# Second attention of a two-layer transformer kernel: the key mask from a table and a bias, the row loads in halves

## The chip, the cores and the metric

One core of one Trainium2 chip runs the whole program in one launch. The metric is the device time of an execution in microseconds (us), the median of several runs.

## The reference

The input is 16 batches of 128 tokens of width 128 (float32), a context of the same shape and a key mask of 16 x 128 integers. Two layers follow one another. Cut to the second attention, which the change is about:

```python
Q = (layernorm(x) @ Wq)   # 16 heads of 8 columns each
K, V = ctx @ Wk, ctx @ Wv
scores = einsum('bhqd,bhkd->bhqk', Q, K) / sqrt(8)
scores = where(mask[:, None, None, :] == 0, -inf, scores)
scores = where(triu(ones, k=1), -inf, scores)        # causal
x = x + einsum('bhqk,bhkd->bhqd', softmax(scores), V) @ Wo
```

Layer 0 is a cross attention without any mask, with biases, and a mixture of 8 experts (two chosen per token) on an RMS-normed input. Layer 1 is the attention above and a feed-forward part with ternary weights and inputs rounded to 8 bits. The drawn mask is all ones.

## The kernel before

Five blocks stand one after the other, each with its own instruction streams for the five engines, and all engines meet between two blocks: `context` (layer 0's projections), `attention` for layer 0, `experts`, `attention` for layer 1 (the second attention), and `ternary_ffn`.

**Rows.** Queries and keys are float32 values split into three bf16 parts. The keys' and queries' parts are stored to DRAM (`k_dram`, `q_dram`) and read back per batch as 72 partition rows (`PRODUCTS`: 3 x 3 parts x 8 columns) into one of four slots (`SLOTS`) of `k_rows` and `q_rows`, for all 16 heads. Rows 96 to 98 hold ones on the keys' side and, on the queries' side, the negated row maxima, which `lay_maxima` (L795) writes by a DMA from `neg_t`. In layer 1 row 72 (`ROW_MASK`) of `k_rows` is the batch's key mask (0 or -1e30 in bf16), which `load_rows` (L116 to L131) fetches by a third DMA from `mask_dram` (L130), against a row of ones in `q_rows` that ACT's queue writes once in `context` (L703). Everything else of the rows is zero.

**One batch of the attention.** It goes in four units q of four heads. `scores` (L852) waits for the batch's rows, then TensorE multiplies 96 rows of `q_rows` and `k_rows` per head into `ps_s` (queries in partitions, L867); in layer 1 a matmul of 512 columns first puts the causal triangle `upper` into the bank (L863). VectorE takes the negated maximum of each query (`maxima`, L957) and splits it in three bf16 parts (`split`, L964 to L970); TensorE turns them (L905), ACT copies them to `neg_t` (L1051), and SP lays them into the rows. Two steps later `shifted_scores` (L884) multiplies all 128 rows the other way round (keys in partitions) into `ps_e`; for units 1 and 3 of layer 1 a matmul with `lower` goes first (L880), for units 0 and 2 GpSimd clears the triangle afterwards (`causal`, L1101). ACT takes the exponential (L1039), TensorE multiplies with the values (`values`, L898), whose tile `v_aug` GpSimd fills (L1092).

**Order of the work.** Step b of an attention does `scores` of batch b+2 beside `shifted_scores` of batch b, unit by unit, and the values of batch b-1. The first and last steps are written out, and steps 6 to 13 are a loop of two turns with four steps each, in which b is a register (all engines but SP in layer 1, whose queue is written out in full). SP's queue per batch is in `load`: in layer 0 it waits for two units of the slot's last user, loads eight heads with two DMAs (`load_half`), waits for the other two units, loads the other half, then lays the maxima of batch b-2. In layer 1 it waits for all four units of batch b-4 (L804), issues keys, queries and mask (L125, L126, L130) and then lays the maxima.

**Experts.** Four groups of four batches, eight experts each. In group 0 TensorE also projects the second attention's keys and values from `ctx_t`, whose last use this is; GpSimd, VectorE and SP split and store the keys (L1208, L1266, L143). In groups 1 to 3 the second attention's queries are made in between: VectorE's statistics of the group (L187, L91 to L101), GpSimd's root (`queries.root`, L195), VectorE's normalising after expert 2 (L200), TensorE's turn after expert 3 (L206). SP then stores the queries of group 0 and loads the rows of the first four batches. All engines work in their order.

Of the kernel before, what the change touches and what calls it, by code (L numbers as in the profile page):

```python
# [14 lines left out]
B = 16  # L15
# [24 lines left out]
ROW_MASK = PRODUCTS  # L40
# [64 lines left out]
def load_half(sp, c, b, r, half):  # L105

    heads, rows_in = slice(half * H // 2, (half + 1) * H // 2), c["rows_in"][half]
    rows, queries = c["k_dram"][0, bass.ds(b, 1)], c["q_dram"][0, bass.ds(b, 1)]
# [7 lines left out]


def load_rows(sp, c, layer, b, r):

    k_rows, q_rows, rows_in = c["k_rows"], c["q_rows"], c["rows_in"][layer]  # L120

    rows, queries = c["k_dram"][layer, bass.ds(b, 1)], c["q_dram"][layer, bass.ds(b, 1)]
    windows = bass.AP(tensor=rows.tensor, offset=rows.offset,
                      ap=[[H * P, PARTS * DK], [DK * H * P, PARTS], [1, H * P]])
    sp.dma_start(k_rows[0:PRODUCTS, r].rearrange("p h t -> p (h t)"), windows).then_inc(rows_in[r], 16)  # L125
    sp.dma_start(q_rows[0:PRODUCTS, r].rearrange("p h t -> p (h t)"),  # L126
                 bass.AP(tensor=queries.tensor, offset=queries.offset,
                         ap=[[H * P, PARTS * DK], [0, PARTS], [1, H * P]])).then_inc(rows_in[r], 16)
    if layer == 1:
        sp.dma_start(k_rows[ROW_MASK:ROW_MASK + 1, r],  # L130
                     c["mask_dram"][bass.ds(b, 1)].unsqueeze(1).to_broadcast([1, H, P])).then_inc(rows_in[r], 16)  # L131
# [256 lines left out]
def main_kernel(nc, t):  # L388
    with ExitStack() as ctx:
        def sb(name, shape, dt):  # L390
# [19 lines left out]
            "ctx_t": sb("ctx_t", [P, T], F32),  # L410

# [14 lines left out]
            "rows_in": [[ctx.enter_context(nc.semaphore(f"rows_in{layer}_{r}")) for r in range(SLOTS)]  # L426
                        for layer in range(2)],
# [7 lines left out]
        c["xr"] = c["tokens"].tk  # L435
        context(nc, t, c)
# [6 lines left out]
def context(nc, t, c):  # L443
# [4 lines left out]
    with ExitStack() as ph:  # L448
# [11 lines left out]
        mask_i, mask_b = sb("mask_i", [B, P], I32), sb("mask_b", [B, P], BF16)  # L460
        one_rows = sb("one_rows", [H, SLOTS * P], BF16)
# [33 lines left out]
        def _(sp):  # L495
# [8 lines left out]
            sp.dma_start(mask_i[:], t["mask"]).then_inc(mask_in, 16)  # L504
            for layer, m in ((0, 3), (1, 0), (1, 1), (1, 2), (1, 3)):
                load_w(sp, layer, m, late_in)
# [9 lines left out]
            for b in range(AHEAD):  # L516
                for half in range(2):
                    load_half(sp, c, b, b, half)
# [611 lines left out]
def experts(nc, t, c):  # L1130
# [6 lines left out]
    with ExitStack() as ph:  # L1137
# [44 lines left out]
        def _(sp):  # L1182
# [12 lines left out]
            for b in range(SLOTS):  # L1195
                load_rows(sp, c, 1, b, b)
# [591 lines left out]
```

## Time and profile before

| | us |
|---|---|
| median of 3 runs | 437.22 (437.04 to 439.81) |
| the profiled execution, its own time | 438.72 |
| its span in the profile | 437.0 |
| TensorE matmul busy | 356.5 (82%) |
| VectorE busy | 288.8 (66%) |
| ACT busy | 224.7 (51%) |
| GpSimd busy | 89.9 (21%) |

Busy times are sums over the span of 437.0 us; the 1.7 us between the span and the execution's own time lie before and after what the profile records. Matmuls overlap their weight loads, so that both columns (PE and PEld) can be busy at once. A wait is the idle time of an engine in front of an instruction, put down to what released it. The granted clock of TensorE was 0.93 of full speed in the mean.

### The profile page before, as it was taken

What the parts mean: (1) busy time and instruction counts of PE and PEld (TensorE: products, weight loads), DVE (VectorE), ACT (ScalarE), POOL (GpSimd) and SP (SyncE); (2) the same over time, 40 slices, a digit from 0 to 9 for tenths busy, and PEclk for the clock granted to TensorE, in tenths of its full rate; (3) what the DMA queues carried; (4) which work ended last, traced back from release to release, by engine and by line L of the source; (5) the groups of instructions that cost most, each with busy time, mean ns of one, the idle gap of its engine ahead of it and who ended that gap; (6) DMA issues with size and microseconds to landing.
All of it is one profiled execution on the core that took longest, in us unless ns stands there. A gap on an engine that the chain in (4) does not pass through costs nothing. (4 is left out here: it accounts for less than half of the span.)

```text
span 437.0 us, 10507 instructions
## 1 busy us (share of the span) xinstructions
PE 356.5 (82%) x3434; PEld 256.6 (59%) x3434; DVE 288.8 (66%) x905; ACT 224.7 (51%) x420; POOL 89.9 (21%) x163
## 2 busy tenths in 40 slices
PE   1484677888977999999999999789899999757663
PEld 0352556766763567776677767557677676534442
DVE  5675677988965753574433443696789899367893
ACT  2142345656664664444434343146566656648894
POOL 6335040020203002100101001124333342310000
PEclk9887599999998999999999999889999999856997
DMA  7555864334317000650161100103444331000111
GB/s 200 119 145 126 209 162 129 118 113 119 97 30 240 2 1 5 127 111 1 35 179 41 36 0 0 37 14 108 132 124 113 96 103 29 3 1 1 32 30 37
DMA packets 54100, 34.98 MB, mean 80 GB/s; under 512 B 38744, under 2 KB 46256, under 8 KB 54064
## 3 DMA queue, kind: packets, MB, share of 16 engines
q1 hardware_dynamic: 44032, 31.43, 26.7%
q10 hardware_dynamic: 10032, 3.08, 3.0%
q8 instruction: 20, 0.33, 0.3%
q14 instruction: 16, 0.13, 0.1%
HBM read 24.60 MB, written 9.44 MB: 78 GB/s over the span
## 5 line engine op out<-in xcount | busy, mean ns | idle before, releaser
L1039 ACT ACTIVATE probs<-ps_e 128x512 f32<-128x512 f32 x128 | 75.5, 594 | 60.7 <-PE ps_e L884 55.9
L957 DVE TENSOR_REDUCE neg<-ps_s 128x4 f32<-128x512 f32 x128 | 85.2, 685 | 23.3 <-PE ps_s L867 22.1
L1285 DVE SCALAR_TENSOR_TENSOR x_all<-ps_ym,c_g,x_all 128x128 f32 (+1 forms) x128 | 36.0, 344 | 63.1 <-PE ps_ym L1380 63.0
L1380 PEld LDWEIGHTS ps_ym<-w,hid 128*128 128x128 f32 x512 | 60.8, 192 | 9.2 <-issue 6.7
L1380 PE MATMUL ps_ym<-w,hid 128*128 128x128 f32 x512 | 62.2, 276 | 0.0
L1370 PE MATMUL ps_h<-tok_t,w 128*128 (+1 forms) x128 | 61.9, 607 | 0.0
L1487 ACT ACTIVATE hid<-ps_h,b 128x512 f32<-128x512 f32 x64 | 43.1, 684 | 35.3 <-PE ps_h L1370 33.9
L867 PE MATMUL ps_s<-k_rows,q_rows 96*128 96x128 bf16 x512 | 54.0, 233 | 8.7 <-PEq L448 3.9
L884 PE MATMUL ps_e<-q_rows,k_rows 128*128 128x128 bf16 x512 | 50.6, 224 | 11.0 <-DMA q_rows<-neg_t 10.3
L867 PEld LDWEIGHTS ps_s<-k_rows,q_rows 96*128 96x128 bf16 x512 | 40.1, 104 | 22.2 <-issue 9.6
L884 PEld LDWEIGHTS ps_e<-q_rows,k_rows 128*128 128x128 bf16 x512 | 36.2, 100 | 17.7 <-DMA q_rows<-neg_t 10.1
L898 PE MATMUL ps_pv<-probs,v_aug 128*32 128x128 f32 x1024 | 36.4, 284 | 0.0
L1370 PEld LDWEIGHTS ps_h<-tok_t,w 128*128 128x128 f32 x128 | 22.5, 195 | 20.1 <-issue 14.9
L1092 POOL TENSOR_TENSOR v_aug<-v_all,zero 128x128 f32<-128x128 f32 x32 | 14.5, 455 | 92.8 <-PE ps_pv L898 92.2
L863 PE MATMUL ps_s<-upper,identb 128*128 128x512 bf16 x64 | 25.8, 404 | 5.1 <-PEq L1137 2.0
L898 PEld LDWEIGHTS ps_pv<-probs,v_aug 128*32 128x32 f32 x1024 | 26.9, 113 | 4.1 <-issue 0.4
L1051 ACT ACTIVATE neg_t<-ps_n 48x128 bf16<-48x128 bf16 x32 | 8.6, 269 | 32.2 <-PE ps_n L905 32.2
L924 PE MATMUL ps_y<-attn_w,oo_t 128*128 128x128 f32 x64 | 15.8, 330 | 9.7 <-ACT oo_t L1056 9.1
L1717 PE MATMUL ps_tf<-ident,gr 128*128 128x128 f32 x64 | 11.8, 313 | 14.0 <-ACT gr L1671 14.0
L983 DVE TENSOR_TENSOR x_all<-ps_y,x_all 128x128 f32<-128x128 f32 (+1 forms) x32 | 9.2, 288 | 17.7 <-PE ps_y L924 17.3
L1101 POOL TENSOR_SCALAR_AFFINE_SELECT probs<-probs 128x512 f32<-128x512 f32 x32 | 20.0, 625 | 0.0
L1044 ACT ACTIVATE o_t<-ps_pv 128x512 f32<-128x512 f32 x32 | 18.6, 580 | 2.0 <-PE ps_pv L898 1.9
(200 smaller groups left out, 552.5 us busy)
## 6 DMA issues: line engine op xcount, KB each, us to landing
k_rows<-k_dram SPq DMA_DIRECT2D x32, 144.0 KB
q_rows<-q_dram SPq DMA_DIRECT2D x32, 144.0 KB
k_rows<-k_dram SPq DMA_DIRECT2D x16, 288.0 KB
q_rows<-q_dram SPq DMA_DIRECT2D x16, 288.0 KB
k_dram<-parts SPq DMA_DIRECT2D x35, 128.0 KB, 2.3
w<-in_w SPq DMA_DIRECT2D x16, 128.0 KB, 2.6
q_dram<-parts SPq DMA_DIRECT2D x15, 128.0 KB, 2.2
q_dram<-parts ACTq DMA_DIRECT2D x9, 128.0 KB, 3.1
```

Source lines behind the costliest of these rows:

```text
L863: pe.matmul(ps_s[:, q % 2, :], identb[:], c["upper"][:].unsqueeze(1).to_broadcast([P, HQ, P]), start=True, stop=False, skip_group_check=True)
L867: last = pe.matmul(ps_s[:, q % 2, j * P:(j + 1) * P], q_rows[0:ROW_MAX, r, h, :], k_rows[0:ROW_MAX, r, h, :], start=(layer == 0), stop=Tru ...
L884: last = pe.matmul(ps_e[:, q % 2, j * P:(j + 1) * P], k_rows[:, r, h, :], q_rows[:, r, h, :], start=not masked, stop=True, skip_group_chec ...
L898: last = pe.matmul(ps_v[VW * j:VW * (j + 1), q * P:(q + 1) * P], v_aug[:, s, q * HQ + j, :], probs[:, s, q, j * P:(j + 1) * P], start=True ...
L957: dve.tensor_reduce(neg[:, s, q * HQ:(q + 1) * HQ], ps_s[:, q % 2, :].rearrange("p (h k) -> p h k", h=HQ), AX_X, ALU.max, negate=True).the ...
L1039: act.activation(probs[:, s, q, :], ps_e[:, q % 2, :], ACT.Exp, scale=SCALE).then_inc(exp_done, 1)
L1044: act.activation(o_t[:, s, :], ps_v[:], ACT.Copy).then_inc(ot_ready, 1)
L1101: pool.affine_select(out=probs[:, s, q, :], in_=probs[:, s, q, :], compare_op=ALU.is_ge, fill=0.0, base=0, pattern=[[0, HQ], [1, P]], chan ...
L1285: dve.scalar_tensor_tensor(out=batch_of(x_all, g * G + j), in0=ps_y[:, e % 2, j * D:(j + 1) * D], scalar=c_g[:, j, e:e + 1], in1=batch_of( ...
L1370: pe.matmul(ps_h[:, m, :], w1[:, e, m * P:(m + 1) * P], tok_t[:, bass.ds(g * GT, GT)], start=True, stop=True).then_inc(h_done, 1)
L1380: last = pe.matmul(ps_y[:, e % 2, j * D:(j + 1) * D], hid[:, (e % 2) * M + m, j * P:(j + 1) * P], w2[:, e, m, :], start=(m == 0), stop=(m ...
L1487: act.activation(hid[:, (e % 2) * M + m, :], ps_h[:, m, :], ACT.Gelu, bias=b1[:, e * M + m:e * M + m + 1]).then_inc(h_ready, 1)
```

## The change

The key mask no longer goes through the rows. In `context` the mask is also read turned round (`mask_t`, 128 keys x 16 batches) and VectorE makes `key_mask` of it (0 or -1e30 per key and batch); ACT's DMA of the row of ones into `q_rows` goes. In `experts`, when the projections have left `ctx_t`, SP fetches `mask_dram` broadcast to 128 partitions (2048 bf16 values in each) into its memory (`masks`) and GpSimd adds `upper` to all sixteen batches, ahead of the queries' part of its queue. In the second attention the matmul at L863 takes the batch's slice of that table instead of `upper`; GpSimd's `fill` copies the batch's column of `key_mask` to `key_bias`, and ACT's exponential takes this as its bias, for which it waits at unit 0. Row loads of layer 1 are done as in layer 0, in halves (four DMAs per batch instead of three), and TensorE waits for a half at units 0 and 2. The `scores` matmuls of both layers take 72 rows instead of 96. The semaphores `rows_in` are now per half; renamings of `rank_ready` are left out below.

```diff
-def load_half(sp, c, b, r, half):
+def load_half(sp, c, layer, b, r, half):
     heads, rows_in = slice(half * H // 2, (half + 1) * H // 2), c["rows_in"][half]
-    rows, queries = c["k_dram"][0, bass.ds(b, 1)], c["q_dram"][0, bass.ds(b, 1)]
+    rows, queries = c["k_dram"][layer, bass.ds(b, 1)], c["q_dram"][layer, bass.ds(b, 1)]
     first, many = half * H // 2 * P, H // 2 * P
...
-def load_rows(sp, c, layer, b, r):
-    k_rows, q_rows, rows_in = c["k_rows"], c["q_rows"], c["rows_in"][layer]
-    rows, queries = c["k_dram"][layer, bass.ds(b, 1)], c["q_dram"][layer, bass.ds(b, 1)]
-    windows = bass.AP(tensor=rows.tensor, offset=rows.offset,
-                      ap=[[H * P, PARTS * DK], [DK * H * P, PARTS], [1, H * P]])
-    sp.dma_start(k_rows[0:PRODUCTS, r].rearrange("p h t -> p (h t)"), windows).then_inc(rows_in[r], 16)
-    sp.dma_start(q_rows[0:PRODUCTS, r].rearrange("p h t -> p (h t)"),
-                 bass.AP(tensor=queries.tensor, offset=queries.offset,
-                         ap=[[H * P, PARTS * DK], [0, PARTS], [1, H * P]])).then_inc(rows_in[r], 16)
-    if layer == 1:
-        sp.dma_start(k_rows[ROW_MASK:ROW_MASK + 1, r],
-                     c["mask_dram"][bass.ds(b, 1)].unsqueeze(1).to_broadcast([1, H, P])).then_inc(rows_in[r], 16)
...
+            "key_mask": sb("key_mask", [P, B], F32),
...
-            "rows_in": [[ctx.enter_context(nc.semaphore(f"rows_in{layer}_{r}")) for r in range(SLOTS)]
-                        for layer in range(2)],
+            "rows_in": [[ctx.enter_context(nc.semaphore(f"rows_in{half}_{r}")) for r in range(SLOTS)]
+                        for half in range(2)],
...
+        c["masks"] = c["ctx_t"][:, 0:T // 2].bitcast(BF16).rearrange("p (b k) -> p b k", b=B)
...
             sp.dma_start(mask_i[:], t["mask"]).then_inc(mask_in, 16)
+            sp.dma_start(mask_t[:], t["mask_t"]).then_inc(mask_in, 16)
...
-                    load_half(sp, c, b, b, half)
+                    load_half(sp, c, 0, b, b, half)
-            sp.wait_ge(rows_set, 16 * (PARTS + 1))
+            sp.wait_ge(rows_set, 16 * PARTS)
...
             dve.tensor_copy(parts[:, FAST, 1], rest[:, FAST]).then_inc(fast_split, 1)
             dve.wait_ge(fast_split, 1)
             dve.tensor_tensor(parts[:, FAST, 2], rest[:, FAST], parts[:, FAST, 1], ALU.subtract).then_inc(fast_split, 1)
-            dve.wait_ge(mask_in, 16)
+            dve.wait_ge(mask_in, 32)
+            dve.tensor_scalar(c["key_mask"][:], mask_t[:], 0, MASKED, ALU.is_equal, ALU.mult)
             dve.tensor_scalar(mask_b[:], mask_i[:], 0, MASKED, ALU.is_equal, ALU.mult).then_inc(mask_ready, 1)
...
                         act.dma_start(k_rows[ROW_MAX + r:ROW_MAX + r + 1], one_rows[:]).then_inc(rows_set, 16)
-                    act.dma_start(q_rows[ROW_MASK:ROW_MASK + 1], one_rows[:]).then_inc(rows_set, 16)
...
+        key_bias, n_filled = sb("key_bias", [P, 2], F32), 1 + layer
-        n_loads = 2 if layer == 0 else 3
...
             def load(b, r):
-                if layer == 0:
-                    for half in range(2):
-                        sp.wait_ge(shifted, (b - SLOTS) * NQ + (half + 1) * NQ // 2)
-                        load_half(sp, c, b, r, half)
-                else:
-                    sp.wait_ge(shifted, (b - SLOTS + 1) * NQ)
-                    load_rows(sp, c, layer, b, r)
+                for half in range(2):
+                    sp.wait_ge(shifted, (b - SLOTS) * NQ + (half + 1) * NQ // 2)
+                    load_half(sp, c, layer, b, r, half)
                 lay_maxima(b - 2, (r - 2) % SLOTS)
...
             def scores(b, q, r):
                 n = b * NQ + q
-                if layer == 0 and q % 2 == 0:
-                    wait(pe, c["rows_in"][q // 2][r], of_slot(b, r, SLOTS, 16 * n_loads))
-                if layer == 1 and q == 0:
-                    wait(pe, rows_in[r], of_slot(b, r, SLOTS, 16 * n_loads) + 16 * 2 * B // SLOTS)
+                if q % 2 == 0:
+                    wait(pe, c["rows_in"][q // 2][r], of_slot(b, r, SLOTS, 16 * 2) + layer * (16 * 2 * B // SLOTS))
                 wait(pe, max_done, n - 1)
-                    pe.matmul(ps_s[:, q % 2, :], identb[:], c["upper"][:].unsqueeze(1).to_broadcast([P, HQ, P]),
+                    pe.matmul(ps_s[:, q % 2, :], identb[:], c["masks"][:, bass.ds(b, 1), :].to_broadcast([P, HQ, P]),
                               start=True, stop=False, skip_group_check=True)
                 for j in range(HQ):
                     h = q * HQ + j
-                    last = pe.matmul(ps_s[:, q % 2, j * P:(j + 1) * P], q_rows[0:ROW_MAX, r, h, :], k_rows[0:ROW_MAX, r, h, :],
+                    last = pe.matmul(ps_s[:, q % 2, j * P:(j + 1) * P], q_rows[0:PRODUCTS, r, h, :], k_rows[0:PRODUCTS, r, h, :],
                                      start=(layer == 0), stop=True, skip_group_check=True)
                 last.then_inc(scored, 1)
...
-                    wait(pe, vaug_ready, b + 1)
+                    wait(pe, vaug_ready, (b + 1) * n_filled)
...
                 wait(act, pv_done, n - 2 * NQ + 1)
-                act.activation(probs[:, s, q, :], ps_e[:, q % 2, :], ACT.Exp, scale=SCALE).then_inc(exp_done, 1)
+                if layer == 1 and q == 0:
+                    wait(act, vaug_ready, (b + 1) * n_filled)
+                masked = key_bias[:, s:s + 1] if layer == 1 else 0.0
+                act.activation(probs[:, s, q, :], ps_e[:, q % 2, :], ACT.Exp, bias=masked, scale=SCALE).then_inc(exp_done, 1)
...
             def fill(b, s):
                 wait(pool, pv_done, (b - 1) * NQ)
+                if layer == 1:
+                    pool.tensor_tensor(key_bias[:, s:s + 1], c["key_mask"][:, bass.ds(b, 1)], c["zero"][:, 0:1], ALU.add)\
+                        .then_inc(vaug_ready, 1)
                 pool.tensor_tensor(v_aug[:, s, :, 0:DK],
...
+            sp.wait_ge(v_done, NG)
+            sp.dma_start(c["masks"][:], c["mask_dram"].unsqueeze(0).to_broadcast([P, B, P])).then_inc(tables_ready, 16)
             queries.store(sp, 0, queries.stored[0])
             sp.wait_ge(queries.stored[0], 16 * PARTS)
             for b in range(SLOTS):
-                load_rows(sp, c, 1, b, b)
+                for half in range(2):
+                    load_half(sp, c, 1, b, b, half)
             queries.store(sp, 1, queries.stored[1])
-            pool.iota(rank_i[:], pattern=[[-1, E]], base=E, channel_multiplier=0).then_inc(rank_ready, 1)
-            pool.wait_ge(rank_ready, 1)
-            pool.tensor_copy(rank[:], rank_i[:]).then_inc(rank_ready, 1)
+            pool.iota(rank_i[:], pattern=[[-1, E]], base=E, channel_multiplier=0).then_inc(tables_ready, 1)
+            pool.wait_ge(tables_ready, 1)
+            pool.tensor_copy(rank[:], rank_i[:]).then_inc(tables_ready, 1)
                 pool.wait_ge(k_copied, 2 * (g + 1))
                 pool.tensor_tensor(k_rest[:, g], k_full[:, g], k_parts[:, g, 0], ALU.subtract).then_inc(k_rest_ready, 1)
+            pool.wait_ge(tables_ready, 2 + 16)
+            pool.tensor_tensor(c["masks"][:], c["masks"][:], c["upper"][:].unsqueeze(1).to_broadcast([P, B, P]), ALU.add)
             with pool.Fori(0, NG - 1) as g:
                 queries.root(pool, g)
                 queries.leave(pool, g)
...
-            dve.wait_ge(rank_ready, 2)
+            dve.wait_ge(tables_ready, 2)
...
-        "mask": mask_BxS2_if1,
+        "mask": mask_BxS2_if1, "mask_t": np.transpose(mask_BxS2_if1),
```

## Rows read from the trace of the kernel before

**Rows 1.** Windows: us, then PE, PEld, DVE, ACT, POOL busy; clock; DMA.

```profile
136.50:279.60 143.10, 139.82 (x788) 97.71 (x788) 71.33 (x258) 65.17 (x101) 13.27 (x13) 0.99 0.20 50
...
279.60:386.80 107.20, 94.55 (x1254) 69.05 (x1254) 82.86 (x257) 60.47 (x130) 37.87 (x88) 0.94 0.27 77
```

**Rows 2.** Waits of the second attention: total us, times, longest.

```profile
PE ps_s L863 <- DMA k_rows<-mask_dram: 1.7, 4, 0.8
...
PEld ps_s L863 <- DMA k_rows<-mask_dram: 1.2, 3, 0.5
```

**Rows 3.** Windows of single steps of the second attention, columns as in 1.

```profile
322.80:328.30 5.50, 5.27 (x78) 4.00 (x76) 5.19 (x20) 3.30 (x7) 2.20 (x6) 1.00 0.35 110
...
339.80:346.20 6.40, 5.54 (x80) 4.22 (x81) 5.17 (x16) 3.39 (x7) 1.94 (x5) 1.00 0.38 99
```

**Rows 4.** Timeline of SP's queue, second attention: start, duration.

```profile
297.75 0.81 SPq L125 DMA_DIRECT2D k_rows<-k_dram  x1
...
334.03 0.81 SPq L125 DMA_DIRECT2D k_rows<-k_dram  x1
...
335.71 0.55 SPq L130 DMA_DIRECT2D k_rows<-mask_dram  x1
...
336.42 0.80 SPq L795 DMA_DIRECT2D q_rows<-neg_t  x1
...
357.50 0.81 SPq L125 DMA_DIRECT2D k_rows<-k_dram  x1
```

**Rows 5.** Timeline of VectorE and TensorE around a late load.

```profile
338.54 0.68 DVE L957 TENSOR_REDUCE neg<-ps_s 128x4 f32<-128x512 f32 x1
...
340.51 0.39 PE L863 MATMUL ps_s<-upper,identb 128*128 128x512 bf16 x1 [0.80 <-DMA k_rows<-mask_dram]
```

**Rows 6.** Instructions of lines L867, L884 and L110: min, median, max ns.

```profile
L867 PEld LDWEIGHTS ps_s<-k_rows,q_rows x512: 95/98/152, 39.1 to 368.2; 96*128 96x128 bf16 x171
...
L884 PEld LDWEIGHTS ps_e<-q_rows,k_rows x512: 95/97/156, 49.9 to 379.7; 128*128 128x128 bf16 x171
...
L110 SPq DMA_DIRECT2D k_rows<-k_dram x32: 772/802/1584, 24.3 to 113.7; - x32
```

**Rows 7.** DMA issues (KB each, us to landing) and GpSimd's largest addition (ns).

```profile
ffn_w<-in_w_gate SPq DMA_DIRECT2D x1, 256.0 KB, 3.1
...
mask_i<-in_mask SPq DMA_DIRECT2D x1, 8.0 KB, 8.7
...
k_dram<-parts SPq DMA_DIRECT2D x35, 128.0 KB, 2.3
...
L1114 POOL TENSOR_TENSOR x_all<-x_all,row_bias x1: 4510/4510/4510, 56.5 to 56.5; 128x2048 f32<-128x2048 f32 x1
```

**Rows 8.** Timeline of the experts at the start of group 1.

```profile
184.67 5.15 SPq L143 DMA_DIRECT2D k_dram<-parts  x9
...
192.25 0.16 DVE L101 SCALAR_TENSOR_TENSOR q_vareps<-q_tmp,q_vareps 128x4 f32<-128x4 f32 x1
...
192.50 1.01 POOL L195 TENSOR_TENSOR q_rstd<-q_vareps,half 128x4 f32<-128x4 f32 x1 [12.45 <-DVE q_vareps L101]
...
197.90 1.11 DVE L200 TENSOR_SCALAR q_xn<-x_all,q_mean,q_rstd 128x128 f32 x4
...
201.34 0.60 PE L206 MATMUL ps_c<-ident,q_xn 128*128 128x128 f32 x4
```

**Rows 9.** A register operation in front of a matmul in a loop (ns).

```profile
L1710 PEldq FUSED_REGOPS  x8: 51/55/65, 408.3 to 423.0; - x8
```

**Rows 10.** Timeline of context: ACT's queue and VectorE.

```profile
12.40 0.61 ACTq L703 DMA_DIRECT2D q_rows<-one_rows  x1
...
21.02 0.21 DVE L615 TENSOR_SCALAR mask_b<-mask_i 16x128 bf16<-16x128 int32 x1
...
21.15 1.10 DVE L594 TENSOR_SCALAR xn<-x_all,mean,rstd 128x128 f32<-128x128 f32 x4
...
27.60 2.76 DVE L594 TENSOR_SCALAR xn<-x_all,mean,rstd 128x128 f32<-128x128 f32 x4
```

More of the change, by code:

```diff
@@ L39 @@
 PRODUCTS = PARTS * PARTS * DK
-ROW_MASK = PRODUCTS
 ROW_MAX = 96
@@ L460, in context @@
         mask_i, mask_b = sb("mask_i", [B, P], I32), sb("mask_b", [B, P], BF16)
+        mask_t = sb("mask_t", [P, B], I32)
         one_rows = sb("one_rows", [H, SLOTS * P], BF16)
@@ L714, in attention @@
     x_all, ident, identb, attn_w = c["x"], c["ident"], c["identb"], c["attn_w"]
-    k_rows, q_rows, rows_in = c["k_rows"], c["q_rows"], c["rows_in"][layer]
+    k_rows, q_rows = c["k_rows"], c["q_rows"]
     with ExitStack() as ph:
@@ L812, in _ @@
                     for half in range(2):
-                        load_half(sp, c, b, b, half)
+                        load_half(sp, c, 0, b, b, half)
             for b in range(2):
@@ L1165, in experts @@
         ps_q = ph.enter_context(nc.psum_tensor("ps_q", [P, GT], F32))
-        x_added, rank_ready, lg_done, lg_ready = sem("x_added"), sem("rank_ready"), sem("lg_done"), sem("lg_ready")
+        x_added, tables_ready, lg_done, lg_ready = sem("x_added"), sem("tables_ready"), sem("lg_done"), sem("lg_ready")
         k_done, k_copied, k_rest_ready, k_split, k_stored, v_done, v_ready = (
```

## Prediction

> **What bounds the kernel now.** I read the windows by stage first, then the waits of the second attention, then single steps of it, and last SP's queue and the other engines around the steps that came out long. The experts' stage, 136.5 to 279.6 us, has TensorE busy in 139.8 of 143.1 us: what delays TensorE there is paid in full. The second attention, 279.6 to 386.8, has TensorE at 94.6 of 107.2 us (88%) and VectorE at 82.9 (77%) [rows 1]. A step of its steady part that waits for nothing takes 5.5 us, with TensorE busy in 5.27 and VectorE in 5.19 of them; the longest of the later steps takes 6.4 with hardly more work in it, 5.54 and 5.17 [rows 3]. So the stage runs at TensorE's pace with VectorE close behind, and what is to be had are the gaps in front of TensorE.
>
> Among the gaps is one that this change touches. The list of waits has TensorE waiting at L863 for the mask row's DMA, 1.7 us in 4 places for the matmul and 1.2 us in 3 more for its weights, 2.9 in all [rows 2]. SP's queue shows why. The load of a slot starts when the fourth unit of its last user is through, at 334.03 for one batch, and the third DMA, the mask, leaves SP at 335.71 + 0.55 = 336.26 [rows 4]. The scores of that batch want it one step later, at about 339.7; they start at 340.51 after 0.80 of waiting, 4.2 us after the issue ended, while VectorE's maximum that they need as well was ready at 338.54 + 0.68 = 339.22 [rows 5]. So 2.2 us of issuing and 3.5 to 4.2 us of landing make about one step of 5.5: the loads arrive on the edge, sometimes before it and sometimes behind.
>
> **The change part by part.** The sum is made against the profiled execution, 438.72 us with a span of 437.0; that execution was 1.5 us above the median of the runs, 437.22, and I take the same difference off the median.
>
> *Loads in halves.* The first half of a slot is now loaded after two units of its last user, half a step (2.7 us) earlier, and the second half, issued where the whole is today, is wanted only at unit 2, half a step later. Both gain about 2.7 us of slack, over three times the longest wait of 0.8, so the 2.9 us [rows 2] end. Not all comes back: part of a weight load's wait lies beside the matmul before it, and VectorE, with 5.19 of 5.5 us busy [rows 3], will be what is late next. I take -2.2. One end is 0, if VectorE takes over every gap. The other: from the load at 297.75 to that at 357.50, the first and last of eleven, ten steps take 59.75 us [rows 4]; ten at 5.46 would be 54.6, so -5.15 if every wait there is in truth this one. SP pays for it: four issues of 0.80 [rows 6] and the maxima's 0.80 [rows 4], 4.0 us and some gaps against 3.0, inside a step of 5.5. The maxima's DMA stands in the same place behind the second half, now with two issues ahead of it after the fourth unit in place of three (1.6 us, not 2.2), and was issued 2.4 us into the step (336.42) because it waits for `neg_t`; it isn't later. The extra packets cost no time that I can see: cost 0. Before the stage, SP issues 16 loads instead of 12, under the experts, ahead of a store that waits for the queries of the next group: 0.
>
> *Mask row gone, triangle from the table.* Same matmul, same columns: 0. But in the eight batches of the loop the moving operand's address is now a register expression, four times each. In the other loop that does this, a register operation of 51 to 65 ns stands before the matmul [rows 9]. 32 of them are 1.8 us at the median 55 ns and 2.1 at 65, if none is hidden; nothing, if TensorE's queue runs ahead, as it mostly does behind matmuls. I take +0.3.
>
> *72 rows instead of 96.* Weight loads of 96 and of 128 rows have medians of 98 and 97 ns [rows 6]: the rows do not count. 24 fewer: 0; with 1 ns each way on 512 loads, 0.5 either way.
>
> *Bias and its column.* The exponential has the same shape and reads a column in place of a constant: 0. GpSimd gets one small operation per batch; it is busy 2.2 us of a step [rows 3] and `fill` runs a whole step before ACT needs it: 0. If that cover went, ACT would wait at unit 0 for some 0.2 us per batch, and its slack of 2 us per step would still hold it.
>
> *The table in the experts.* SP's last key store ends at 184.67 + 5.15 = 189.82; then comes the table's DMA. 256 KB landed 3.1 us after issue and stores of 128 KB 2.3 [rows 7], 0.8 more per 128 KB, so 512 KB about 4.7: landed at 194.6. The addition has 128x2048 elements, and GpSimd's addition of that size took 4.51 us [rows 7]: done at 199.1. Behind it in GpSimd's queue stands the first root of the queries, 192.50 now, 1.01 us; it moves to 199.1 and ends at 200.1. VectorE would start normalising at 197.90 and now waits 2.3 us, then needs 1.11; TensorE wants the result at 201.34 [rows 8]. 201.3 against 201.34: the slack is used up to the last tenth. I take +0.5 for what comes on top (the semaphores, the stores in front). Ends: 0, and, if the table lands as slowly as the mask's small load, 8.7 us [rows 7], at 198.6, so that everything is 4.0 later, +4.0.
>
> *Context.* One more VectorE operation beside the 0.21 us of the mask [rows 10], on the path of the normalised input, some 0.1 to 0.2; one DMA of 128 short rows among the first loads; one issue of 0.61 less on ACT [rows 10], whose next copy is covered by TensorE anyway. I take +0.2; ends -0.4 and +1.0.
>
> Sum: -2.2 + 0.3 + 0.5 + 0.2 = -1.2. The profiled execution would be 437.5, the median 437.22 - 1.2 = 436.0. All low ends together give -6.0 (431.2), all high ends +7.6 (444.8).
>
> A rule that speaks against the table: the Trainium skill (SBUF — State Buffer, on the shared port pair) says that GpSimd and VectorE take the pair as an exclusive lock, held for a whole instruction, when VectorE runs in a fast mode or reads two SBUF operands. The trace agrees: four normalisations of 1.10 us in all took 2.76 beside GpSimd's work [rows 10]. What it would do here is the fourth rival.
>
> **The rivals.**
> 1. *The table is late (slower).* Its DMA lands after 8.7 us instead of 4.7: GpSimd's root, VectorE's normalising and TensorE's turn move by 4.0 beyond the slack. For it: 512 KB, all from the same 4 KB of DRAM, behind five stores. Against it: the 3.1 us of the weights' load [rows 7]. -2.2 + 0.3 + 4.0 + 0.2 = +2.3: 439.5; where VectorE also keeps the gain of the loads, +4.5: 441.7. It decides from a landing about 1.7 us later than I take, where it outweighs the gain of 1.2. Chance 0.13.
> 2. *The gap changes its name.* The loads come in time and TensorE waits for VectorE's maxima instead. For it: VectorE's 5.19 of 5.5. Against it: at 340.51 the maximum was 1.3 us old [rows 5]. 0 + 1.0: 438.2. Chance 0.15.
> 3. *The loads set more than the rows tell.* Steps of 5.8 us without a named wait are late loads too, and all come down to 5.46: -5.15 + 1.0 = -4.1: 433.1. Chance 0.10.
> 4. *GpSimd's addition locks VectorE out.* If the table landed 2.3 us after issue, at 192.2, the addition would start in the middle of the group's variance, which ends at 192.41 [rows 8], and hold its last operation until 196.7, 4.3 us, of which TensorE's slack of about 1 us hides a part: +3.3 in place of +0.5, so +1.6: 438.8. Only a narrow stretch of landing times does it. Chance 0.04.
> 5. *Register operations in full*, 2.1 instead of 0.3: +0.6: 437.8. Chance 0.08.
>
> **How the numbers follow.** The forecast has 0.50. A measurement of this kernel tells about 1% from no change, 4.4 us. Faster by that needs all of rival 3 and something more: 0.08. Slower by that needs rival 1 in its worse form, or two costs together: 0.12. Within 1%: 0.80. The range holds rivals 2 to 5 and most of rival 1: 432.9 to 439.8.
>
> **What would show it.** In the changed profile: no wait of TensorE at L863's matmul for a row load in the steady part, and steps near 5.5 us; SP's first half of a load issued in mid-step; weight loads of 72 rows at 98 ns; an addition of some 4.5 us on GpSimd from about 194.6, the root behind it ending near 200, and TensorE's first turn of the queries near 201.5 to 202. The prediction is wrong if the steps stay at 5.8 with VectorE named as releaser, if the experts' stage grows by over 1.5 us, or if register operations appear before L863 with idle time.

## The result, and the profile after

The kernel after takes 442.05 us in the median of 7 runs (440.66 to 443.29), the kernel before 438.48 in as many runs beside it (437.04 to 439.95): a ratio of 1.0092, with a 95% interval of 1.0063 to 1.012. The change makes the kernel slower by 0.9%, 3.6 us, where 1.2 us less were forecast.

The windows of the same two stages, the experts and the second attention by its own ends (279.7 to 386.1 before, 278.4 to 387.8 now), against [rows 1]:

```profile
136.50:278.40 141.90, 139.55 (x787) 97.58 (x786) 70.22 (x252) 65.20 (x101) 17.02 (x13) 0.99 0.20 50
278.40:387.90 109.50, 97.91 (x1254) 71.49 (x1254) 81.76 (x256) 64.69 (x128) 40.40 (x104) 0.91 0.26 75
279.00:296.00 17.00, 14.90 (x123) 9.71 (x121) 13.40 (x40) 5.69 (x9) 4.44 (x12) 0.60 0.21 50
296.00:320.00 24.00, 21.58 (x257) 15.94 (x255) 15.04 (x38) 13.44 (x27) 9.00 (x23) 0.86 0.33 96
```

All of the loss is in the second attention, which takes 109.5 us instead of 106.4. (The two profiled executions are only 1.9 us apart, 440.66 and 438.72 us: these 3.1 less the 1.3 by which the stage began earlier, see below.) Three more busy microseconds of TensorE are in it for the same 1254 matmuls, and the granted clock of the stage is 0.91 where it was 0.94. The last two rows say where: in its first 17 us the mean clock is 0.60, and in the next 24 it is 0.86. The same two windows of before:

```profile
279.00:296.00 17.00, 14.09 (x141) 9.32 (x142) 13.98 (x43) 6.28 (x12) 5.95 (x13) 0.80 0.20 48
296.00:320.00 24.00, 21.79 (x311) 16.07 (x308) 17.53 (x49) 13.45 (x29) 8.58 (x21) 1.00 0.42 117
```

Cut finer, the clock of before stands at 0.50 (1.2 GHz) for 6.8 us from 281.3 and then, until 373, at 1.00 (2.4 GHz). After, it stands at 0.50 for 13.7 us from about 279.7 and for 6.8 more from about 310.7. Two single microseconds of before, then two of after, show the ends of the first stretch:

```profile
281.00:282.00 1.00, 0.81 (x6) 0.68 (x7) 0.73 (x2) 0.00 (x0) 0.55 (x2) 0.69 1.05 216
289.00:290.00 1.00, 0.20 (x2) 0.17 (x3) 0.92 (x4) 0.32 (x1) 1.00 (x4) 1.00 0.00 0
```

```profile
280.00:281.00 1.00, 1.00 (x6) 0.64 (x7) 0.40 (x1) 0.00 (x0) 0.45 (x2) 0.50 1.03 232
292.00:293.00 1.00, 1.00 (x7) 0.63 (x6) 0.41 (x2) 0.69 (x1) 0.08 (x1) 0.50 0.33 45
```

TensorE did 18 matmuls less in the first 17 us.

What the forecast said of the waits came true. TensorE's waits in the second attention (engine, what, for what; total us, times, longest) have no row load of any kind, against the mask's 1.7 us in [rows 2]:

```profile
PE ps_y L904 <- ACT oo_t L1039: 6.4, 13, 1.5
PE ps_s L843 <- PEq L1123: 2.0, 1, 2.0
PE ps_s L843 <- DVE neg L937: 1.6, 2, 1.1
PE ps_n L885 <- DVE neg_parts L950: 1.5, 2, 1.0
PE ps_y L900 <- DVE o L958: 0.8, 1, 0.8
PE ps_e L864 <- ACT probs L1022: 0.7, 1, 0.7
```

And SP's queue (start, us), with one step from 326.91 to 332.46, issues the second halves there and the first halves in mid-step, at 329.95; most steps of the steady part take 5.55 us and the longest 6.1, where before's queue, of which [rows 4] shows some lines, has 5.4 to 6.4 there:

```profile
326.91 0.78 SPq L109 DMA_DIRECT2D k_rows<-k_dram  x1
327.73 0.78 SPq L112 DMA_DIRECT2D q_rows<-q_dram  x1
329.13 0.77 SPq L782 DMA_DIRECT2D q_rows<-neg_t  x1
329.95 0.80 SPq L109 DMA_DIRECT2D k_rows<-k_dram  x1
330.80 0.78 SPq L112 DMA_DIRECT2D q_rows<-q_dram  x1
332.46 0.78 SPq L109 DMA_DIRECT2D k_rows<-k_dram  x1
```

One thing came out smaller. The register operation that the forecast looked for in front of L863 (now L843) is there, once in each of the eight batches of the loop and not four times (shortest, median and longest ns), and no idle time is put down to it:

```profile
L843 PEldq FUSED_REGOPS  x8: 46/48/51, 325.6 to 366.3; - x8
```

The table in the experts does as forecast too. In the timeline SP issues it at 188.37, GpSimd adds when it has landed, and root and normalising follow, against [rows 8]:

```profile
188.37 0.51 SPq L1178 DMA_DIRECT2D ctx_t<-mask_dram  x1
192.96 4.06 POOL L1200 TENSOR_TENSOR ctx_t<-ctx_t,upper 128x2048 bf16<-128x2048 bf16 x1 [14.24 <-DMA ctx_t<-mask_dram]
196.97 1.02 POOL L178 TENSOR_TENSOR q_rstd<-q_vareps,half 128x4 f32<-128x4 f32 x1
198.03 1.11 DVE L183 TENSOR_SCALAR q_xn<-x_all,q_mean,q_rstd 128x128 f32 x4 [1.37 <-POOL q_rstd L178]
200.02 0.60 PE L189 MATMUL ps_c<-ident,q_xn 128*128 128x128 f32 x4
```

This stage ends 1.3 us earlier than before's (278.4 against 279.7), and was already 1.3 us ahead when it began (the context's block ended 2.0 us earlier in this execution, and the first attention gave part of that back): the table costs nothing that shows here.

One group of the page (line, engine, names, shapes; count; busy us, mean ns) changed that the forecast had at nothing. The exponentials of the second attention, with the bias column, and those of the first, without:

```profile
L1022 ACT ACTIVATE probs<-ps_e,key_bias 128x512 f32<-128x512 f32 x64 | 43.8, 687 | 31.8 <-PE ps_e L864 26.9
L1022 ACT ACTIVATE probs<-ps_e 128x512 f32<-128x512 f32 x64 | 37.4, 593 | 29.0 <-PE ps_e L864 28.8
```

A bias from a column costs 94 ns per exponential. So there were two suspects, the 72 rows (by the clock, since the durations are the same) and the bias, and perhaps a gain by the halves hidden under them.

### The profile page after: what moved, and what is told of

Read it like the earlier page. It is cut to its first block and busy times, and to the rows that moved or that the text cites. A ratio compares the mean times of both kernels' runs of the same rounds, so it can differ in the third digit from the quotient of the medians.

```text
span 438.9 us, 10580 instructions
## 1 busy us (share of the span) xinstructions
PE 360.0 (82%) x3434; PEld 258.9 (59%) x3434; DVE 288.2 (66%) x906; ACT 230.1 (52%) x420; POOL 96.7 (22%) x180
## 5 line engine op out<-in xcount | busy, mean ns | idle before, releaser
L847 PE MATMUL ps_s<-k_rows,q_rows 72*128 72x128 bf16 x512 | 54.9, 235 | 9.2 <-DVE neg L937 4.3
L864 PE MATMUL ps_e<-q_rows,k_rows 128*128 128x128 bf16 x512 | 51.5, 227 | 10.9 <-DMA q_rows<-neg_t 9.0
L1022 ACT ACTIVATE probs<-ps_e,key_bias 128x512 f32<-128x512 f32 x64 | 43.8, 687 | 31.8 <-PE ps_e L864 26.9
L847 PEld LDWEIGHTS ps_s<-k_rows,q_rows 72*128 72x128 bf16 x512 | 40.6, 105 | 23.7 <-issue 11.4
L1022 ACT ACTIVATE probs<-ps_e 128x512 f32<-128x512 f32 x64 | 37.4, 593 | 29.0 <-PE ps_e L864 28.8
L843 PE MATMUL ps_s<-ctx_t,identb 128*128 128x512 bf16 (+1 forms) x64 | 27.2, 425 | 4.0 <-PEq L1123 2.0
L904 PE MATMUL ps_y<-attn_w,oo_t 128*128 128x128 f32 x64 | 16.0, 332 | 9.9 <-ACT oo_t L1039 9.8
```

Of the source, the lines that this page charges most:

```text
L843: pe.matmul(ps_s[:, q % 2, :], identb[:], c["masks"][:, bass.ds(b, 1), :].to_broadcast([P, HQ, P]), start=True, stop=False, skip_group_che ...
L847: last = pe.matmul(ps_s[:, q % 2, j * P:(j + 1) * P], q_rows[0:PRODUCTS, r, h, :], k_rows[0:PRODUCTS, r, h, :], start=(layer == 0), stop=T ...
L864: last = pe.matmul(ps_e[:, q % 2, j * P:(j + 1) * P], k_rows[:, r, h, :], q_rows[:, r, h, :], start=not masked, stop=True, skip_group_chec ...
L1022: act.activation(probs[:, s, q, :], ps_e[:, q % 2, :], ACT.Exp, bias=masked, scale=SCALE).then_inc(exp_done, 1)
```

## The experiments

Times are medians; a ratio is to the runs of the kernel before of the same session (438.08, 437.90, 437.94 and 437.83 us in the four sessions, each on another chip), with its 95% interval. It is worked out over the runs and isn't the quotient of the two medians, from which it differs by up to 0.24%. Where two variants are compared, their ratios are divided and the half widths added in squares.

**One part undone, one part alone.** From the kernel after, the bias out of the exponentials or the rows back at 96:

```diff
-                masked = key_bias[:, s:s + 1] if layer == 1 else 0.0
+                masked = 0.0                                            # a_nobias
...
-   q_rows[0:PRODUCTS, r, h, :], k_rows[0:PRODUCTS, r, h, :],
+   q_rows[0:ROW_MAX, r, h, :], k_rows[0:ROW_MAX, r, h, :],              # a_rows96
```

> The changed kernel with the constant 0.0 as the bias of all exponentials; GpSimd's column and ACT's wait stay. It leaves the key mask out of the exponentials. Theory A (the bias column makes each of the 64 exponentials 0.09 us longer, ACT is what TensorE waits for where the queries are finished inside the second attention, and the longer holes let the granted clock fall): the exponentials go back to about 0.594 us, the second low-clock stretch near 311 us goes, and the time falls from 442.0 to 437 to 439. Theory B (the 72 rows lower the clock): stays at 442. Theory C (halves of loads run TensorE into longer holes): stays at 442, with exponentials of 0.594 us.

> The changed kernel with the scores over 96 rows again (rows 72 to 95 are zero in the queries' rows). Theory B: the clock's low stretches shrink to those of the kernel before and the time falls to 437 to 439. Theories A and C: nothing changes, 442 within 1.

From the kernel before, a zero column as bias in the second attention, or the loads in halves, the mask row split with them (six DMAs per batch):

```diff
+   ACT.Exp, bias=(c["zero"][:, 0:1] if layer == 1 else 0.0), scale=SCALE)      # b_bias
...
+    if layer == 1:                                                             # b_halves, in load_half
+        sp.dma_start(c["k_rows"][ROW_MASK:ROW_MASK + 1, r, heads],
+                     c["mask_dram"][bass.ds(b, 1)].unsqueeze(1).to_broadcast([1, H // 2, P])).then_inc(rows_in[r], 16)
```

> The kernel before with a column of zeros from a tile as the bias of the second attention's 64 exponentials, in place of the constant. Theory A: exponentials of 0.687 us and a time of 440 to 442, against 438.5 for the kernel before. Theories B and C: exponentials may be longer but the time stays within 1 us of before, since ACT has over 2 us of idle time in a step.

> The kernel before with the row loads of the second attention in halves, the mask row's DMA split likewise (six DMAs per batch). Theory C: 440 to 442, with a second low-clock stretch near 311 us. Theories A and B: the waits for the mask row's DMA go (2.9 us in the trace before) and the time is 435.5 to 437.5; if SP's six issues per batch (4.3 us and the maxima's 0.8 in a step of 5.5) get in the way, no gain.

Measured: without the bias 438.12 us, 0.9996 (0.9971 to 1.0022). With 96 rows 437.83, 0.9997 (0.9969 to 1.0025). The bias on the kernel before 439.66, 1.0043 (1.0013 to 1.0073), its exponentials at 686 ns. The halves alone 435.75, 0.9923 (0.9888 to 0.9958). So each of three parts acts by itself: the halves gain 0.8%, and taking away either the bias or the 72 rows brings the kernel after back to the time of before, not below it. Neither suspect alone is the cause; both are.

No theory came out whole. Without the bias the second stretch at 1.2 GHz, near 311 us, was shorter in the profile (3.4 us for 6.8) but not gone, as theory A wanted; with 96 rows it was gone. The halves alone had one of 3.4 us there too, at 435.75 us, so that stretch doesn't tell the kernels apart. The bias on the kernel before, 439.66, stayed below the 440 to 442 of theory A and above what B and C left room for.

**Do they add up?** The kernel after once more; with both undone (a_nobias_rows96: halves, table and `key_bias` column stay); and each cost put on the kernel with halves (bh_bias, bh_rows; the row for the mask is the 73rd, so the second attention takes 73).

> The changed kernel unaltered, beside its variants on this chip. The first measurement had 442.05 against 438.48 for the kernel before, while leaving out the bias column or going back to 96 rows gave about 438 each. If both parts cost something only together (theory D: each adds to the chance of a low-clock stretch), it stays at 441 to 443. If the first measurement caught an unlucky spell of the clock (theory E), it comes out at 438 to 440.

> The changed kernel with both undone: constant bias (the key mask is left out of the exponentials) and 96 rows. What is left is the halves, the table and GpSimd's column. If the table costs nothing it equals the kernel before with halves, 435.5 to 436.5; each us above that is the table's cost (my prediction took 1.0 for table, register operations and the rest).

> The kernel before with halves (435.75) and a column of zeros as the bias of the second attention's exponentials. If the bias costs what it did without halves (438.08 to 439.66), 437 to 438; if the halves leave ACT as what is late (theory A in its stronger form), 439 or more.

> The kernel before with halves and the scores over 72 rows in the first attention and 73 in the second (the mask row is the 73rd) instead of 96. Theory B: 438 or more, with longer low-clock stretches. Otherwise 435.75 within 0.7.

| | median us | ratio (95%) | mean clock of its runs |
|---|---|---|---|
| after, again | 441.59 | 1.0072 (1.0040 to 1.0104) | 0.912 |
| both undone | 434.51 | 0.9925 (0.9890 to 0.9959) | 0.931 |
| halves + bias | 437.44 | 0.9982 (0.9954 to 1.0010) | 0.923 |
| halves + 72/73 rows | 437.41 | 1.0005 (0.9975 to 1.0034) | 0.919 |

Both undone is as fast as the halves alone (0.9925 against 0.9923): the table, its addition, the register operations, the column's fill and the context together cost nothing that is measured here, within 0.5%. That is a balance, since the halves alone have the mask's two DMAs per batch besides; v_keep below has neither them nor the table and comes out at 0.9928, so neither shows within this noise. The bias costs 0.6% on the kernel with halves (0.9982 / 0.9923) and 0.7% on the kernel after (0.9997 / 0.9925), the rows 0.8% and 0.7% (1.0005 / 0.9923, 0.9996 / 0.9925), each with some 0.45% either way. -0.75 + 0.7 + 0.7 gives +0.7%, and the kernel after shows +0.7 and +0.9%. The run with the rows, 437.41 us, stayed a little under the 438 of theory B.

**Which attention, and how many rows?** All on the kernel with halves: 72 rows in the first attention alone, 73 in the second alone, and 32 in both.

```diff
-   q_rows[0:ROW_MAX, r, h, :], k_rows[0:ROW_MAX, r, h, :],
+   q_rows[0:(ROW_MAX if layer == 0 else ROW_MASK + 1), r, h, :], ...    # bh_rows_l1
+   q_rows[0:(32), r, h, :], k_rows[0:(32), r, h, :],                    # bh_rows32
```

> The kernel before with halves, scores over 72 rows in the first attention only, 96 in the second. The whole cut cost 437.7 against 435.2 (means) with a mean granted clock of 0.919 against 0.927, although each matmul and weight load takes the same time. Theory B (the clock is granted less where fewer rows take part): about half of it, 436 to 437, if both attentions have a share; 435.2 within 0.7 if only the second one does.

> The counterpart: 96 rows in the first attention, 73 in the second. Theory B: the rest of the 2.5 us; 436 to 437, or 437.7 if only the second attention matters. If both of these come out at 435.2 the cut's cost was chance.

> The kernel before with halves and the scores over 32 rows only in both attentions, which leaves out the products of rows 32 to 71 and the mask row. Theory B: more than the 2.5 us of the cut from 96 to 72 rows, 439 or more, with a mean clock of 0.91 or less and matmuls of the same duration. If rows do not matter: 435.2 within 0.7 and a clock of 0.927.

Measured: first attention alone 434.81 us, 0.9944 (0.9918 to 0.9969); second alone 437.63, 1.0013 (0.9987 to 1.0038); 32 rows 449.05, 1.0254 (1.0215 to 1.0293). The cost of 72 or 73 rows is the second attention's. It isn't in the durations. Weight loads of the steady part, 322 to 370 us, with 96, 73 and 32 rows:

```profile
L863 PEld LDWEIGHTS ps_s<-k_rows,q_rows 96*128 96x128 bf16 x132 | 10.2, 97 | 4.0
```

```profile
L863 PEld LDWEIGHTS ps_s<-k_rows,q_rows 73*128 73x128 bf16 x131 | 10.1, 97 | 4.0
```

```profile
L863 PEld LDWEIGHTS ps_s<-k_rows,q_rows 32*128 32x128 bf16 x128 | 7.1, 92 | 9.3 <-issue 9.3
```

96 and 73 are alike. With 32 there is a second cost of another kind: these loads have 9.3 us of idle time before them with no releaser named. From an `upper` matmul, which has 128 rows, to the first product of 32 rows behind it TensorE goes on after 0.31 us instead of 0.22, and from the four products to a matmul of 128 rows behind them after 0.33 instead of 0.22. Eight steps of the steady part take 6.05 us in the mean instead of 5.49 (most of them 6.07 instead of 5.46); the stage takes 116.9. 16 steps by 0.56 are 9.0 of the 13.6 us by which the stage is longer than with the halves alone, so that run says little about the clock. Its first low-clock stretch was nevertheless the longest of all, 17.1 us.

**Where in the stage? First four batches against the other twelve.** The profiles so far suggested that what differs is the length of the first stretch at 1.2 GHz behind the stage's start. The test puts 73 rows, or the bias, in batches 0 to 3 alone, or in all but these:

```diff
+   ROW_MASK + 1 if layer == 1 and isinstance(b, int) and b < 4 else ROW_MAX          # bh_rows_first4
+   ROW_MASK + 1 if layer == 1 and not (isinstance(b, int) and b < 4) else ROW_MAX    # bh_rows_last12
```

> The kernel before with halves in the second attention, and there 73 rows in the score products of batches 0 to 3 alone (64 of 256 products), 96 elsewhere. Theory A (fewer rows lengthen the stretch of granted clock 0.50 at the stage's start, from some 7 to some 13.5 us, and nothing else): the whole cost of the 73 rows, +2.2 to +3 us on the kernel with halves, 437.5 us; the profile's first low stretch after 279 us is some 13.5 us long. Theory B (each product, or each step, with fewer rows costs a little): a quarter of it, 435.5 to 436 us.

> The complement: 96 rows in batches 0 to 3 of the second attention, 73 in batches 4 to 15. Theory A: as the kernel with halves alone, 434.8 to 435.5 us, first low stretch some 7 us. Theory B: three quarters of the cost, 436.9 to 437.3 us.

> The kernel before with halves, the column of zeros as bias in the exponentials of batches 0 to 3 of the second attention alone (16 of 64). Theory A (slower exponentials lengthen the low stretch at the stage's start): +2 us, 437.2 us, first low stretch 13.5 us. Theory B (each of the 64 exponentials, 0.094 us longer, delays TensorE in the steady steps too): a quarter, 435.7 us.

> The complement: the column in the exponentials of batches 4 to 15 (48 of 64). Theory A: as the kernel with halves alone, 434.8 to 435.5 us, first low stretch some 7 us. Theory B: three quarters of the cost, 436.7 us.

| on the kernel with halves | median us | ratio (95%) |
|---|---|---|
| 73 rows, batches 0 to 3 | 438.08 (436.23 to 439.32) | 1.0006 (0.9982 to 1.0030) |
| 73 rows, batches 4 to 15 | 434.90 (431.78 to 437.30) | 0.9948 (0.9905 to 0.9992) |
| bias, batches 0 to 3 | 434.99 (433.31 to 436.68) | 0.9941 (0.9909 to 0.9974) |
| bias, batches 4 to 15 | 436.39 (434.65 to 439.19) | 0.9969 (0.9938 to 1.0000) |

For the rows theory A holds: 64 of the 256 products carry the cost, 192 carry at most a small part. All runs, and not only the profiled ones, show the clock in it: their mean granted clock is 0.919 with the 73 rows in batches 0 to 3 and 0.928 with them in the others, 0.009 apart, give or take 0.004. For the bias it falls: the first four batches cost nothing that shows, and what there is of a cost is in the twelve later ones, though the two bias runs alone (1.0028, give or take 0.0045) don't separate them.

The windows of the stage's first 17 us, of 73 rows in batches 0 to 3 and of 96 there (the run with the bias in the same batches):

```profile
279.00:296.00 17.00, 15.04 (x121) 10.03 (x125) 13.24 (x40) 5.41 (x9) 4.69 (x10) 0.60 0.19 48
```

```profile
279.00:296.00 17.00, 14.04 (x141) 9.33 (x142) 13.91 (x43) 6.60 (x12) 5.92 (x13) 0.80 0.21 51
```

These are the numbers of after and before over again: 0.60 and 121 matmuls against 0.80 and 141. TensorE's waits from 276 to 296 us are all but the same in both, so no wait explains the lower clock:

```profile
PE ps_s L859 <- PEq L1133: 2.0, 1, 2.0
PE ps_n L901 <- DVE neg_parts L966: 1.4, 2, 0.8
PE ps_s L859 <- DVE neg L953: 0.5, 1, 0.5
```

```profile
PE ps_s L859 <- PEq L1133: 2.0, 1, 2.0
PE ps_n L901 <- DVE neg_parts L966: 1.7, 2, 1.1
PE ps_s L859 <- DVE neg L953: 0.5, 1, 0.5
```

In all profiles: with 72 or 73 rows in batches 0 to 3 the first low stretch of the second attention lasted 13.7 us in five (after, after again, a_nobias, bh_rows_l1, bh_rows_first4) and 6.8 in one (bh_rows); with 96 rows there 6.8 us in nine and 13.7 in two (bh_bias, bh_rows_last12). So the rows don't fix its length; they shift the odds. The runs agree: those of bh_rows_first4 all lie above 436.2, while those of bh_rows_last12 and of the halves alone spread from about 432 to 438.

The stage's length, from SP's store at its start to the end of the last output projection, sorts the profiles with halves and at least 72 rows:

| first low stretch | no bias | bias (all, or batches 4 to 15) |
|---|---|---|
| 6.8 us | 102.6, 102.8, 103.0, 103.1, 103.2, 103.3 | 104.2, 106.0 |
| 13.7 us | 104.8, 106.1, 106.4, 106.5 | 107.4, 109.5, 109.5 |

The entry of 103.0 has the bias in batches 0 to 3; one of the two of 109.5 is the profile of bh_bias, the slowest of that kernel's twelve runs (441.07 us). In the means the longer stretch stands for some 3 and 3.6 us, down the two columns, and the bias for 2.1 and 2.8, along the two rows.

**What the bias costs.** a_nobias_rows96 and a_rows96 differ in the bias alone, and both have a first low stretch of 6.8 us. Their steady steps are 5.46 and 5.55 us: one exponential's 94 ns per step, although a step has four and ACT is idle for a third of it. TensorE's waits from 322 to 366 us, without and with:

```profile
PE ps_y L904 <- ACT oo_t L1039: 0.6, 3, 0.3
```

```profile
PE ps_y L904 <- ACT oo_t L1039: 1.5, 5, 0.6
```

And ACT's timeline of one step with the bias:

```profile
334.71 0.58 ACT L1027 ACTIVATE o_t<-ps_pv 128x512 f32<-128x512 f32 x1
335.50 0.69 ACT L1022 ACTIVATE probs<-ps_e,key_bias 128x512 f32<-128x512 f32 x1 [0.21 <-PE ps_e L864]
336.09 0.27 ACT L1039 ACTIVATE oo_t<-ps_y 128x128 f32<-128x128 f32 x1
336.29 0.69 ACT L1022 ACTIVATE probs<-ps_e,key_bias 128x512 f32<-128x512 f32 x1
```

The copy of `oo_t`, which TensorE needs for L904, stands in ACT's queue behind one exponential, itself released by TensorE at 335.50. What that exponential gains in length, TensorE waits: it starts L904 at 336.41 after 0.24 us. 16 steps by 0.09 are 1.4 us of the 2 to 3. bh_bias shows the longer step as well. Two starts of the same matmul, one step apart, with the halves alone (5.46 us) and with the bias too (5.55):

```profile
325.17 0.23 PE L901 MATMUL ps_n<-identb,neg_parts 128*128 128x128 bf16 x1
330.63 0.23 PE L901 MATMUL ps_n<-identb,neg_parts 128*128 128x128 bf16 x1
```

```profile
327.62 0.23 PE L901 MATMUL ps_n<-identb,neg_parts 128*128 128x128 bf16 x1
333.17 0.23 PE L901 MATMUL ps_n<-identb,neg_parts 128*128 128x128 bf16 x1
```

The rest goes with a lower clock, as far as the runs tell. In all four pairs of kernels that differ in the bias of all 64 exponentials alone, the mean granted clock of the runs is lower with it:

| with and without the bias | mean clock |
|---|---|
| b_bias, the kernel before beside it | 0.922, 0.927 |
| bh_bias, b_halves | 0.923, 0.927 |
| a_rows96, a_nobias_rows96 | 0.923, 0.931 |
| after again, a_nobias | 0.912, 0.923 |

The differences are 0.004 to 0.011, each with some 0.005 either way; together they come to 0.007, give or take 0.003. (Only the first pair ran on one chip; the kernel before had 0.927 to 0.929 on all four.) And a straight line through the fifteen stages of the table above, in the time that each stood at 1.2 GHz (8.6 to 22.7 us in all) and in the share of its exponentials that have the bias, gives 0.38 us for each us at the lower level and 1.6 us, give or take 0.5, for the bias beside it: an estimate from single executions, but it is the 1.4 us of the steps. By the same line the 6.9 us by which the first stretch can be longer are worth 2.6 us. Why longer exponentials should lower the clock no run tells.

**A version without both.** Halves, 96 rows, no mask row, no table and no bias: the key mask as 0 or 1 multiplies the values and the column of ones in GpSimd's fill. The maxima are then taken over masked keys as well, which drops out of the softmax unless every unmasked score lies so far below a masked one that its exponential underflows.

```diff
+                    pool.tensor_tensor(v_aug[:, s, :, DK:DK + 1], c["ones"][:, 0:H].unsqueeze(2),
+                                       keep.to_broadcast([P, H, 1]), ALU.mult).then_inc(vaug_ready, 1)
+                    pool.tensor_tensor(v_aug[:, s, :, 0:DK], v_b, keep.to_broadcast([P, H, DK]), ALU.mult)\
+                        .then_inc(vaug_ready, 1)
```

> A candidate that keeps only what paid: halves, 96 rows, no bias, no mask row and no table; the key mask (1 or 0 per key) multiplies the values and the column of ones that makes the sums, in GpSimd's fill, and the maxima are taken over all causal keys. Four DMAs per batch. If the table cost nothing and the mask row's DMAs cost nothing, it is where halves alone and the changed kernel without bias and cut were, 434 to 436; two of GpSimd's operations per batch instead of one should be hidden.

Measured: 434.44 us, 0.9928 (0.9902 to 0.9955). It beats both kernels, by no more than the halves alone do; the steady steps are at 5.46.

## Why the prediction was wrong

**What bounds the kernel: right.** The gaps in front of TensorE were what was to be had; the loads' waits ended and the steady steps fell to about 5.5 us. None of the three signs that the prediction gave for being wrong came (steps of 5.8 us behind VectorE, a longer experts' stage, register operations with idle time), and it was wrong all the same: none of them watched the length of an exponential or the clock.

**Loads in halves, -2.2: right in sign and mechanism, perhaps undersized.** Alone they give -3.4 us by the ratio (0.9923 of 438; its interval, -1.8 to -4.9, holds the -2.2) and -2.3 by the two medians, inside the ends of 0 and -5.15. "VectorE ... will be what is late next" didn't come: in the steady part of after, 322 to 350 us, VectorE waits for TensorE's scores (1.5 us), and of TensorE only weight loads wait for VectorE's maxima (0.5 us).

**72 rows, "the rows do not count: 0": the step that failed.** It rests on [rows 6], which are right and still hold, 97 ns each. What they can't tell is the clock under which they run. The windows had the clock in their last columns, 0.94 in the second attention [rows 1], and the working took it as given; nothing in it allowed an edit to change it. Four comparisons have +0.6 to +0.8%, 2.5 to 3.6 us, as far as can be told all from the start of the second attention. The bounds, 0.5 us either way, held only the durations. The Trainium skill (TensorE: Matmul & The Clock Gate, on the step-by-step phases of a matmul) says that a weight load's time goes by the columns and the number of rows doesn't matter; the trace agrees on the duration, 97 ns for 96 and for 73 rows. The time of the kernel changed all the same.

**Bias and its column, "reads a column in place of a constant: 0": the other step that failed.** +0.4 to +0.7% in three comparisons, 1.9 to 3.2 us, of which some 1.4 are longer steps and the rest goes with a lower clock. This one was to be read from the trace of before, in two of ACT's groups that read the same shape from PSUM, one with a bias column and one without (they write different types; L1466, bf16 without a column, took 597 ns):

```profile
L696 ACT ACTIVATE parts<-ps_p,attn_bias 128x512 bf16<-128x512 f32 x8 | 5.5, 686 | 11.4 <-PE ps_p L667 6.6 <-PE ps_p L655 4.8
L684 ACT ACTIVATE xn_t<-ps_x 128x512 f32<-128x512 f32 x4 | 2.4, 594 | 8.2 <-PE ps_x L636 8.2
```

92 ns, 64 times: 5.9 us of ACT. The second half of the step, that ACT's idle 2 us per step would hold it, failed as well: the idle time lies elsewhere in the step than the exponential that the copy of `oo_t` stands behind. The Trainium skill (ScalarE: Activation LUTs, on what a table load costs) gives 93 ns for each operand of one column; the trace agrees, with these 92 ns and the exponentials' 94.

**Register operations, table, context: +1.0 forecast, 0 measured** (0.9925 against 0.9923, within 0.5%). The table's landing was right: 4.5 us after its issue by the page of the profile, for an estimate of 4.7. The addition took 4.06 and not 4.51. Everything was 2.1 us earlier than forecast at the addition's end (197.0 for 199.1), of which 1.3 are the lead that the stage came with; the root ended at 198.0 and TensorE turned at 200.0. Rival 1 (a late table), rival 4 (the lock) and rival 5 (the register operations) didn't happen. Rival 2, VectorE in the place of the loads, didn't either.

**The sum.** -3.3 for the halves, about 0 for table and all around it, some +3 for the rows and some +2.7 for the bias: +2.4, where the two measurements have +3.6 and +3.7 by their medians (+4.0 and +3.2 by the ratios). The forecast had -2.2, +1.0, 0 and 0. Another part of the miss is its base: the kernel before was taken at 437.22, the median of 3 runs, and had 438.48 over 7, which is 1.3 of the 6.0 us between 436.0 and 442.05. None of the rivals was the one that came: all of them moved waits and none moved a duration or the clock. That two terms were called 0 without a bound, or with one from durations alone, also made the range too narrow: it ended at 439.8.

## What to carry to other kernels

Before an edit that changes an operand's kind is put at nothing, look for two groups of the same shape in the trace, one with a column and one with a constant, and then find which instruction stands behind it in the engine's queue; an idle share of a third doesn't hide it. Where a stage runs part of its time at the lower clock level, an edit to TensorE's work at its start can change how long that lasts with every duration unchanged: compare the clock column of the windows, in several executions, before and after. Splitting the loads of a slot paid here; change one thing at a time, since three effects of 0.7% each, of both signs, look like one small one.

## What was not expected of the hardware

- Products of 72 or 73 rows instead of 96, with the same durations (97 ns for the weight load) and the same waits, in 64 matmuls at the start of a stage: the stretch at 1.2 GHz lasted 13.7 us in five of six profiles, against two of eleven with 96 rows, and the kernel took 0.6% longer than with these rows in the other 192 products. Why the rows should matter to the clock no run here tells; that they do is shown by bh_rows_first4 against bh_rows_last12 (1.0058, give or take 0.0049).
- Products of 32 rows beside matmuls of 128 rows: 0.1 us more at a change from the one to the other, either way (0.31 to 0.33 us from start to start instead of 0.22), and 0.56 us per step of four units. With 73 rows the steps had no such cost.
- A bias column in ACT's exponentials, 0.09 us longer each: the mean granted clock of TensorE over the runs was 0.004 to 0.011 lower in four pairs of kernels, beside the time that TensorE waits for ACT.
- The time of one and the same kernel spreads by over 1% (the halves alone 432.7 to 438.0 us), and follows the mean granted clock of the run: in the kernel with 73 rows in batches 4 to 15 the four fastest runs had 0.931 to 0.935, the others 0.923 to 0.927.
